# Flamingo gated block on one core: moving the query eviction ahead of four exponentials on ScalarE

## What is computed

```python
def xattn(h, ctx):                       # h = layernorm(x)
    q, k, v = h @ Wq, ctx @ Wk, ctx @ Wv # inner width 1024 = 16 heads x 64
    scores = einsum('bhsd,bhkd->bhsk', q, k) / 8
    probs = softmax(scores)
    return einsum('bhsk,bhkd->bshd', probs, v) @ Wo + bo

x = x + tanh(g_xattn) * xattn(layernorm(x), ctx)
logits = layernorm(x) @ gate_w.T         # 8 experts, the two best of each token
# tokens get slots in their experts; out = gates * (relu(xe @ fc1 + b1) @ fc2 + b2)
x = x + tanh(g_ffn) * moe(layernorm(x))
```

## Time and profile before

| | |
|---|---|
| median of 3 runs | 991.46 us (989.94 to 992.4) |
| the profiled execution | 994.87 us |
| its span in the profile | 993.1 us |
| granted TensorE clock, mean | 0.983 of full speed |

### The profile page before, as it was taken

One profiled execution on the slowest core, in us unless ns is written; L12 is line 12 of the kernel. 1 busy time (PEld: TensorE's weight loads), 2 busy tenths in 40 slices (PEclk: granted clock), 3 DMA queues, 4 the chain that ended last, 5 costly groups with the idle time before them and its releaser, 6 DMA issues.

```text
span 993.1 us, 18998 instructions
## 1 busy us (share of the span) xinstructions
PE 949.4 (96%) x7199; PEld 823.4 (83%) x7199; DVE 676.3 (68%) x1542; ACT 508.1 (51%) x1573; POOL 281.8 (28%) x293
## 2 busy tenths in 40 slices
PE   7799999999999999999999888999999999999996
PEld 5587877888878878878888786999999999999995
DVE  5768687686785886886776862757575665657572
ACT  3567376465664773673754621535444343435352
POOL 6803025024033043042041133222222223232222
PEclk8989999999999999999999998999999999999998
DMA  9096003011020021021011015254342435252521
GB/s 259 22 298 194 22 2 107 23 41 67 22 86 24 22 92 38 2 86 44 1 44 44 13 52 187 66 117 101 76 128 50 128 49 130 49 130 56 141 53 22
DMA packets 63099, 76.63 MB, mean 77 GB/s; under 512 B 6033, under 2 KB 55096, under 8 KB 63008
## 3 DMA queue, kind: packets, MB, share of 16 engines
q1 hardware_dynamic: 50720, 59.18, 20.0%
q0 software_dynamic: 12288, 16.23, 9.0%
HBM read 46.52 MB, written 29.49 MB: 77 GB/s over the span
## 4 chain that ended last, share of the span: by engine, by line
PE 73%; ACT 11%; DVE 8%; POOL 3%; DMA 2%; issue 2%; SPq 1%; POOLq 0%; DVEq 0%; another core or an unknown queue 0%
PE down L1211 6%; PE down L1210 6%; PE down L1209 6%; PE up L1195 6%; PE up L1196 6%; PE up L1197 6%; PE score L545 4%; ACT probs_odd L733 4%; ACT work L733 4%; PE out_bank L533 4%; PE probT L520 4%; DVE negmax L913 2%; PE rT L1179 2%; PE query_bank L466 2%; PE query_bank L464 2%
## 5 line engine op out<-in xcount | busy, mean ns | idle before, releaser
L1151 POOL DMA_INDIRECT out_dram<-eo,index x64 | 99.4, 1553 | 282.2 <-ACT eo L1253 250.4
L1245 ACT ACTIVATE hid<-up,b 128x512 f32<-128x512 f32 x128 | 88.3, 690 | 84.8 <-PE up L1197 84.8
L733 ACT ACTIVATE probs_odd<-score,negmax 128x128 f32<-128x128 f32 x256 | 91.3, 382 | 44.6 <-DVE negmax L913 44.6
L733 ACT ACTIVATE work<-score,negmax 128x128 f32<-128x128 f32 x256 | 91.4, 383 | 42.8 <-DVE negmax L913 42.8
L407 POOL DMA_INDIRECT disp<-packed,slots x64 | 68.8, 1075 | 133.8 <-DVE slots L904 92.4
L913 DVE TENSOR_REDUCE negmax<-score 128x4 f32<-128x512 f32 x128 | 82.0, 682 | 28.1 <-PE score L545 27.7
L698 ACT ACTIVATE k_sb<-key_bank 128x512 f32<-128x512 f32 x64 | 38.8, 606 | 112.8 <-PE key_bank L489 111.5
L1253 ACT ACTIVATE eo<-eo_raw,gate 128x256 f32<-128x256 f32 x64 | 30.9, 506 | 122.4 <-DVE eo_raw L1315 122.4
L1306 DVE TENSOR_TENSOR hid_l<-hid,hid_h 128x512 fp32r<-128x512 f32 x128 | 88.6, 693 | 4.4
L921 DVE COPY pT<-probT 128x512 f32<-128x512 f32 x128 | 82.2, 682 | 8.7 <-PE probT L520 7.4
L1315 DVE TENSOR_TENSOR eo_raw<-down,b 128x256 f32<-128x256 f32 x64 | 25.8, 423 | 86.4 <-PE down L1211 86.4
(11 more groups left out here) (253 smaller groups left out, 2788.8 us busy)
## 6 DMA issues: line engine op xcount, KB each, us to landing
rows<-disp SPq DMA_DIRECT2D x18, 516.0 KB, 5.4
w_raw<-fc1T_dram SPq DMA_DIRECT2D x9, 1024.0 KB, 8.3
w_raw<-fc_dram SPq DMA_DIRECT2D x9, 1024.0 KB, 10.9
disp<-fixed SPq DMA_DIRECT2D x1, 8256.0 KB, 33.8
rows<-x_dram SPq DMA_DIRECT2D x16, 512.0 KB, 4.3
out_dram<-rows SPq DMA_DIRECT2D x8, 512.0 KB, 3.1
c_raw<-ctxT_dram SPq DMA_DIRECT2D x8, 256.0 KB
c_raw<-ctxT_dram SPq DMA_DIRECT2D x16, 128.0 KB
```

What stands on the lines that cost most here:

```text
L733: last = nc.scalar.activation(probs[w % 2][:, c, :], score[hh][:, b * P:(b + 1) * P], ACT.Exp, bias=negmax[:, w % 2, c:c + 1], accum_out=s ...
L1151: pool.indirect_dma_start(out=out_rows[:, :], out_offset=bass.IndirectOffsetOnAxis(ap=index[half][:, i:i + 1], axis=0), in_=eo[half][:, i, ...
L1245: nc.scalar.activation(hid[m % 2][:, :], up[m % 2][:, :], ACT.Relu, bias=b1[par][:, m:m + 1]).then_inc(s_hid, 1)
```

## The change

ScalarE's `step` waits for q_ready and evicts q directly behind `aT_h`, and makes the second four exponentials of the previous pair after that. The same instructions run, with the same waits, on all engines; only their order on ScalarE is another, in every step from u = 1.

```diff
                 exponentials(u - 1, 0)
             if u > 2:
                 attention_high(u - 3)
+            act.wait_ge(s_q_ready, u + 1)
+            high(q_sb[:, :], query_bank[:, :], SCALE).then_inc(s_q_done, 1)
             if u > 0:
                 exponentials(u - 1, 1)
-            act.wait_ge(s_q_ready, u + 1)
-            high(q_sb[:, :], query_bank[:, :], SCALE).then_inc(s_q_done, 1)
             if "XA" in kinds:
```

## The result

| | before | after |
|---|---|---|
| median | 990.4 us (989.94 to 992.4, 5 runs) | 1000.89 us (999.5 to 1002.15, 5 runs) |
| ratio | | 1.0107, interval 1.0095 to 1.0118 |
| profiled execution, its span | 994.87, 993.1 us | 1002.15, 1000.3 us |

The changed kernel is slower by 1.07%. The forecast was slower too, but by 3.6 us, to 995.1 with a range up to 999.5; the loss is near 10 us. The direction was right and the size was not. (The forecast started from a median of 991.46; with two more runs it is 990.4.) The granted clock is no part of it: over the stretch from 26 to 560 us it was 0.99 of full speed in both profiles.

What follows compares the result with a forecast made beforehand. TensorE was busy 949.4 of 993.1 us, but VectorE was taken to set the length of most steps. The terms -2.8 - 3.2 + 6.6 + 6.2 - 3.4 + 0.2 = +3.6 on 991.46 gave 995.1 us, range 988.5 to 999.5.

Steps and rivals of the forecast that it cites:

- The loop and its release: Maxima, exponentials, `aT_h`, q and scores form a loop; the scores' release doesn't move, as q plus second exponentials take as long.
- Steps 0 to 2: Scores, values and projection: 0 for the first two steps, 0.2 us for group 0, 2.8 us won at the projection.
- Steps 3 and 4: `XA`, `XB` and `LT` on TensorE: 0.1 and 0.3 us won, 0.9 in the last group, 3.2 us won.
- Step 5: ScalarE waits for the late query, exponentials start 1.35 us late, maxima move 0.94 in seven groups: 6.6 us lost.
- Step 6: VectorE's additions meet GpSimd's `split_ctx`: 0.95 to 1.45 us, 1.2 taken, in five groups, 0.1 in two: 6.2 us lost.
- the tie: VectorE's second division and GpSimd's `split_ctx` start together at 350.50; maxima come after 8.2 us with VectorE first, 8.75 with GpSimd.
- Step 7: TensorE ahead, `xT_l` bound by VectorE's own division: 0.53 us in five groups, 0.8 in the sixth, 3.4 us won.
- A: Rival: no meeting with GpSimd in step 6, which costs 0.8 us in all instead of 6.2: 989.7 us; chance 0.24.
- D: Rival: step 5 costs nothing, the routing chain isn't what the maxima wait for: 988.5 us; chance 0.08.
- B: Rival: worse meeting with GpSimd in step 6, three additions caught: up to 8 us on top, 1003; chance 0.11.
- C: Rival: TensorE doesn't get ahead in step 7, so the 3.4 us are not won: 998.5 us; chance 0.13.
- E: Rival: nothing that counts changes, gains and losses vanish alike in waits for each other: 991.5 us; chance 0.06.

Runs made afterwards that it cites:

- second profile: The kernel before, unchanged, run and profiled once more: 992.79 us, ratio 0.9997, profile span 990.2 us.
- last experiment: The kernel before with the new order in steps 0, 1 and 2 alone, groups 1 to 7: 994.96 us beside 995.56, ratio 0.9992.

## Why the prediction was right or wrong

**The loop and its release**: right. Scores start where they did in step 5, 5.60 after the maxima, since q and the second exponentials together are as long as they were.

**Steps 0 to 2: this is the step that failed.** The prediction put 0 on steps 0 and 1, because "what it waits there for scores or TensorE's slack in step 2 takes that up", and 2.8 won on step 2 by the wait for q of the earlier trace rows. Both were read off an execution with nine late signals. A late signal sets the length of its step, lets TensorE get ahead of VectorE and so into a wait for q, and hides VectorE's delay. In the second profile step 2's projection starts behind the values from group 2 on, so nothing is there to be won.

And VectorE's delay in step 1 is more than "0.48 less room": there too the query is late, as in step 5. In the changed kernel:

```profile
304.16 0.60 ACT L698 ACTIVATE q_sb<-query_bank 128x512 f32<-128x512 f32 x1 [0.55 <-PE query_bank L466]
...
306.19 0.18 DVE L926 RECIPROCAL rsum<-sums 128x4 f32<-128x4 f32 x1 [1.15 <-ACT work L733]
```

ScalarE waits 0.55 in every group from 1 to 6 and 0.74 in the last, and VectorE starts on the second half 5.29 after the maxima (300.90) instead of 4.24 in the second profile; its row statistics and the maxima come behind that. The first profile could not show this, since its late signal had put TensorE ahead: the last query matmul of step 1 started 1.99 after the maxima (299.85 - 297.86), against 3.01 in the second profile and 2.83 in the changed kernel. Steps 0 and 1 get longer by 0.27 and 0.71, and only 0.69 of it is TensorE's slack in step 2. That is 0.29 lost a group, 1.7 us in six, instead of 2.8 won: 4.5 of the some 6.5 us by which the forecast was short. The rest is 1.0 in step 6, 0.6 in the last step and 0.5 in steps 3, 4 and 7, less 0.2 in step 5.

The baseline was mixed as well. The forecast took off the 3.4 us by which the profiled execution was over the median, but kept the 2.8 that were to be won on it. The second profile's last maxima are 3.2 us earlier than the first's, and its steps 0 to 2 of groups 2 to 7 are 3.3 shorter in all. Held against the first profile itself, the changed kernel wins 1.55 us in these steps. The 1.7 lost holds against the second profile; by time it is not confirmed, as the last experiment says. A hint was in the rows: the wait of 2.2 us was spread over only 4 of 7 groups that do the same.

**Steps 3 and 4**: 3.2 won forecast (its terms, 0.4 in six groups and 0.9, make 3.3), 2.8 measured: 0.13 and 0.24 in six groups, 0.73 less 0.15 in the last.

**Step 5**: right. 0.94 in seven groups forecast, 0.92 measured, and the experiment with the new order there alone costs its 6.2 us.

**Step 6**: right in mechanism and nearly in size: 0.95 to 1.45 forecast with 1.2 taken, 1.44 measured (8.71 against 7.27) in five groups, 7.2 us, and nothing in the two without a split. VectorE won the tie, for which the forecast had 0.95; it had not counted that the copy of `running` waits as well (0.39 instead of 0.17). That this puts one addition more behind the start of c_l is argued from the lengths. But the tie, of which the prediction made so much, decides little: the old order in step 5 takes it away and the additions still meet c_l.

The Trainium skill (SBUF — State Buffer, Who interferes with whom) says that a VectorE copy can run in a mode that uses the port pair shared with GpSimd, if its operands meet that mode's conditions, and can then contend with GpSimd. The trace agrees, 0.39 us in the changed kernel and 0.43 with the old order in step 5 for a copy that takes 0.17 alone.

**Step 7**: right, 8.34 for 8.35, by the bound that was named: VectorE's `xT_l` follows its own division. One part was wrong. The prediction had `FA` and `FB` no longer wait for q, and TensorE is so far ahead that its wait grew from 0.2 to 0.8; it costs nothing, since ScalarE takes `xT_h` only behind the exponentials.

```profile
360.16 0.66 PE L512 MATMUL query_bank<-ident,rows 128*128 128x128 f32 x4 [0.81 <-ACT q_sb L698]
```

That the gain needs TensorE's lead, from a longer step 6, is shown by the kernel with the old order in step 6 and no split there: 9.16, nothing won. Not costed was the last step, 7.23 for 6.66; with the old order in it, it is 6.66 again.

```profile
565.31 1.29 DVE L913 TENSOR_REDUCE negmax<-score 128x4 f32<-128x512 f32 x2
572.54 1.28 DVE L913 TENSOR_REDUCE negmax<-score 128x4 f32<-128x512 f32 x2
```

The second profile of before:

```profile
556.43 1.29 DVE L913 TENSOR_REDUCE negmax<-score 128x4 f32<-128x512 f32 x2 [0.17 <-PE score L545]
563.09 1.28 DVE L913 TENSOR_REDUCE negmax<-score 128x4 f32<-128x512 f32 x2
```

By the last maxima the changed kernel is 9.45 us later; its medians are 10.5 and 9.7 over those of before. Up to step 10 the two profiles are level, for what DMAs and the first iteration differ by between executions, and the loss grows from there: four groups at 1.76, 1.4 in group 1, 0.1 in group 6, which has no split, and 1.2 in group 7. Of the rivals, A and D didn't come; B named the place where the loss is, but what is lost there is the step's upper case (1.44 for 1.45) and not B's 8 us on top; C's time, 998.5, was near and its mechanism wrong; E is out. That the forecast's direction was right rests on steps 5 and 6, and these were costed well.

## What to carry to other kernels

An eviction moved ahead of independent work on an in-order engine pays for its wait with everything behind it: look at when its input is ready in each kind of step, and use the new order only in those where it is and where the engine that waited for it sets the time. Before a wait in a profile is entered as a gain, see that it comes back in each repetition of the loop; one that is there in 4 of 7 like iterations may be this execution's and not the kernel's. And when an engine falls back by half a microsecond, look at what GpSimd runs there: moving its block to a stretch where VectorE idles was worth 0.27% in the kernel before, as much as the new order in its best steps alone (0.25%), and over 1% in the changed kernel; both together gave 0.64% on the same chip.

## What the runs showed of the hardware

The time from TensorE's first score matmul to the start of an idle VectorE that waits for the scores differs between two profiles of the same program: 2.36 or 1.08 us. From group 2 on the longer time was seen in steps 0 and 1 alone, in which GpSimd's indirect DMAs to the slots run, and in some groups of an execution and not in others. It came with the old order and with mixed ones, not in the two profiles of the changed kernel. Three of the four profiles that have it were taken on one chip, the fourth on a chip that is not on record, and the changed kernel was not profiled on that one chip. No run took the indirect DMAs away, so what causes it stays open.

Four additions of 16 columns, 0.80 us on a free VectorE, took 1.48 or 2.59 beside GpSimd's operations of 0.6 to 1.3 us. How long a tiny operation waits is set by the one it meets.
